# Three attention layers: scores of two units in one run, their maximum and difference in one VectorE operation each

## The reference

```
scores = einsum('bhid,bhjd->bhij', q, k) / sqrt(32)     # per sequence and head: 128 x 128
p      = softmax(scores)                                # layer 1: masked keys
out    = einsum('bhij,bhjd->bhid', p, v)                # layer 0: scaled per head, plus a field term
x      = x + out.reshape(B, S, E) @ Wo.T                # layer 1: normalised before it is added
```

## Time and profile before

| | us |
|---|---|
| median of 3 executions (2985.6 to 2991.92) | 2991.61 |
| the profiled execution's own time | 2992.51 |
| its span, first to last instruction | 2990.7 |
| TensorE busy | 2902.6 |
| VectorE busy | 2048.1 |
| ScalarE busy | 1367.8 |
| attention, about | 70 to 1896 |

### The profile page before, as it was taken

One profiled execution on the slowest core, in us unless ns is written; L12 is line 12 of the kernel. 1 busy time (PEld: TensorE's weight loads), 2 busy tenths in 40 slices (PEclk: granted clock), 3 DMA queues, 4 the chain that ended last, 5 costly groups with the idle time before them and its releaser, 6 DMA issues. The chain is left out here.

```text
span 2990.7 us, 69862 instructions
## 1 busy us (share of the span) xinstructions
PE 2902.6 (97%) x27255; PEld 2520.4 (84%) x27255; DVE 2048.1 (68%) x3640; ACT 1367.8 (46%) x2226; POOL 666.8 (22%) x563
## 2 busy tenths in 40 slices
PE   6999999999999999989999999899999999999998
PEld 5899999998888898878888888688888888888886
DVE  5788788876788888888777778654444465655554
ACT  3555545544566666656666666422222232222221
POOL 1222222221121111133222333122222221111111
PEclk8999999999999999999999999899999999999999
DMA  3444444457544444575443435411212240111101
GB/s 139 95 128 123 128 131 116 129 125 188 142 99 101 105 109 100 130 169 136 105 109 105 112 102 120 153 57 57 71 56 67 78 137 29 43 57 42 56 28 43
DMA packets 514586, 300.45 MB, mean 100 GB/s; under 512 B 411776, under 2 KB 484608, under 8 KB 513952
## 3 DMA queue, kind: packets, MB, share of 16 engines
q1 hardware_dynamic: 514464, 298.76, 37.4%
HBM read 139.31 MB, written 58.72 MB: 66 GB/s over the span
## 5 line engine op out<-in xcount | busy, mean ns | idle before, releaser
L747 PE MATMUL att_bank_a<-keep_hh,keep_wgateh 128*128 128x256 f32 x1536 | 453.1, 295 | 4.8 <-ACT att_af L913 2.3
L748 PE MATMUL att_bank_a<-keep_hh,keep_wgatel 128*128 128x256 f32 x1536 | 434.3, 283 | 0.0
L749 PE MATMUL att_bank_a<-keep_hl,keep_wgateh 128*128 128x256 f32 x1536 | 434.0, 283 | 0.0
L962 ACT ACTIVATE att_shifted<-att_shifted,keep_lift 128x512 f32<-128x512 f32 x384 | 276.6, 720 | 299.2 <-DVE att_shifted L1126 295.7
L1710 DVE TENSOR_TENSOR mlp_act_t<-mlp_bank_u,mlp_sg 128x512 f32<-128x512 f32 x128 | 88.5, 692 | 453.0 <-ACT mlp_sg L1616 449.3
L1122 DVE TENSOR_REDUCE att_top<-att_bank_s 128x4 f32<-128x512 f32 x384 | 264.1, 688 | 182.2 <-PE att_bank_s L798 180.8
L1759 POOL TENSOR_TENSOR mlp_al<-mlp_act_t,mlp_ah 128x512 fp32r<-128x512 f32 x128 | 174.9, 1367 | 870.3 <-ACT mlp_ah L1622 870.3
L1616 ACT ACTIVATE mlp_sg<-mlp_bank_g 128x512 f32<-128x512 f32 x128 | 76.6, 598 | 626.3 <-PE mlp_bank_u L1540 626.1
L957 ACT ACTIVATE att_pq<-att_shifted 128x512 f16<-128x512 f32 x384 | 241.2, 628 | 201.4 <-DMA att_pt<-att_pq 195.3
L747 PEld LDWEIGHTS att_bank_a<-keep_hh,keep_wgateh 128*128 128x128 f32 x1536 | 293.0, 191 | 16.4 <-DVE att_xres L1097 2.8
L748 PEld LDWEIGHTS att_bank_a<-keep_hh,keep_wgatel 128*128 128x128 f32 x1536 | 294.1, 191 | 0.1
(11 more groups left out here) (268 smaller groups left out, 7257.4 us busy)
## 6 DMA issues: line engine op xcount, KB each, us to landing
resid<-att_xres SPq DMA_DIRECT2D x47, 512.0 KB, 2.8
keep_xin<-resid SPq DMA_DIRECT2D x33, 512.0 KB, 3.8
mlp_res<-resid SPq DMA_DIRECT2D x32, 512.0 KB, 4.6
att_xres<-resid SPq DMA_DIRECT2D x31, 512.0 KB, 4.3
mlp_xf<-resid SPq DMA_DIRECT2D x30, 512.0 KB, 4.6
keep_xin<-in_x SPq DMA_DIRECT2D x16, 512.0 KB, 4.5
att_xres<-in_x SPq DMA_DIRECT2D x16, 512.0 KB, 3.8
keep_spare<-in_w_next SPq DMA_DIRECT2D x16, 512.0 KB, 3.9
```

What stands on the lines that cost most here:

```text
L747: nc.tensor.matmul(out, w_h, x_h, start=first, stop=False)
L748: nc.tensor.matmul(out, w_l, x_h, start=False, stop=False)
L749: return nc.tensor.matmul(out, w_h, x_l, start=False, stop=last)
L962: nc.scalar.activation(shifted[:, u % 2], shifted[:, u % 2], ACT.Exp, bias=k["lift"][:, 0:1], scale=SCALE).then_inc(exp_done, 1)
```

## The change

Two slots become one double slot d = 0 to 5; the two units of a double slot share one q/k chunk and differ in the sequence b.

- TensorE makes the scores of both units in one run of 24 matmuls into twice the columns of `bank_s`, in layer 1 behind 4 mask matmuls of 256 columns in place of 8 of 128. It waits once per pair for `shift_done` of the pair before. It weighs both units of a pair together, in all bodies (before: in layer 2 and in the last two groups of layers 0 and 1 one unit in each slot), at the head of double slots 2 to 5. The small jobs move behind the pieces of the even slot. `spans` is another list where there are 8 fills.
- VectorE takes the maximum of both units in one operation, and the difference in one; the difference waits for `low_probs` of both units of the pair before.
- ScalarE does exponential and high part of the first unit, then of the second.
- VectorE's list in a double slot: read the fills of the even slot, shift the pair, (d = 2: coherence factor), normalise the pair of d - 2, low part of the first unit, small jobs, read the fills of the odd slot, low part of the second unit, rest. `normalise(i, 3)` is now in d = 5 of its own group, and `add_field(i - 1, 1)` behind the first shift.
- The buffers stay as they are, and so do GpSimd's and SyncE's lists.

In the diff the first `for d` loop is ScalarE's, the second VectorE's.

```diff
+PAIRS = UNITS // 2
...
-        bank_s = ctx.enter_context(nc.psum_tensor("att_bank_s", [P, 4, 512], F32))[:, :, 0:P]
+        bank_s = ctx.enter_context(nc.psum_tensor("att_bank_s", [P, 4, 512], F32))[:, :, 0:NB * P]
...
-            spans = [2,2,1,1,2,2,2,2,2,2,1,1] if len(fills) == 10 else [2,2,1,1,1,2,2,1,1,1,1,1]
+            if len(fills) == 10:
+                spans = [2, 2, 1, 1, 2, 2, 2, 2, 2, 2, 1, 1]
+            else:
+                spans = [2, 2, 2, 2, 1, 1, 1, 1, 1, 1, 1, 1] if lay(i) < 2 else [2, 2, 2, 1, 2, 1, 1, 2, 1, 1, 1, 0]
...
+            def scores(i, c):
+                if positive(PAIRS * i + c):
+                    pe.wait_ge(shift_done, PAIRS * i + c)
...
+                for b in range(NB):
+                    at = slice(b * P, (b + 1) * P)
+                    for step, (q_t, k_t) in enumerate(((qh, kh), (qh, kl), (ql, kh))):
+                        for h in range(4):
...
+                            mm = nc.tensor.matmul(bank_s[:, h, at], q_t[rows, c, at], k_t[rows, c, at], ...
...
+                for s in range(0, SLOTS, 2):
...
+                        scores(i, s // NB)
                     if s >= 4:
+                        for u in (s - 4, s - 3):
                             weigh_values(i, u)
+                    if s == 6 and lay(i) == 0:
+                        sum_values(i, 0)
+                    if s == 10:
+                        turn_output(i, 0)
                     if not at_last:
                         project_pieces(pieces[s])
+                    if s == 0 and not (isinstance(i, int) and i == 0):
+                        turn_output(i - 1, 1)
+                    if s == 2 and lay(i) == 0:
+                        for b in range(NB):
+                            coherence(i, b)
+                    if norms(i) and s == 8:
+                        norm_sums(i)
+                    project_pieces(pieces[s + 1])
...
+                for d in range(SLOTS // 2):
+                    s = 2 * d
+                    if d == 0:
+                        for b in range(NB):
+                            first_values(i, b)
...
+                    read_fills(s)
+                    if d == 1 and has_x(i, 1):
+                        high_x(i + 1)
...
+                        for u in (s, s + 1):
+                            exponentials(i, u)
...
+                            high_probs(i, u)
+                    if d == 0 and positive(i):
+                        high_output(i - 1, 1)
...
+                    read_fills(s + 1)
+                    if d == 0:
                         for b in range(NB):
                             second_values(i, b)
+                    if d == (3 if post(i) else 2) and pre(i):
...
                         squares(norm_turn(1, i + 2), landing(i + 2))
...
+            def shift_scores(i, c):
+                n = PAIRS * i + c
+                src = bank_s.rearrange("p h (b j) -> p h b j", b=NB)
                 dve.wait_ge(s_full, n + 1)
+                nc.vector.reduce_max(top[:].rearrange("p b h -> p h b"), src, AX_X).then_inc(top_ready, 1)
                 dve.wait_ge(top_ready, n + 1)
+                if positive(NB * n):
+                    dve.wait_ge(p_low, NB * n)
+                peaks = top[:].rearrange("p b h -> p h b").unsqueeze(3).broadcast_to([P, 4, NB, P])
+                nc.vector.tensor_tensor(shifted[:].rearrange("p b h j -> p h b j"), src, peaks, ALU.subtract).then_inc(shift_done, 1)
...
+                for d in range(SLOTS // 2):
+                    s = 2 * d
+                    if s >= UNITS:
+                        normalise(i, d - 2)
+                    read_fills(s)
+                    if s < UNITS:
+                        shift_scores(i, d)
+                        if d == 0 and positive(i) and lay(i - 1) == 0:
+                            add_field(i - 1, 1)
+                    if d == 2 and lay(i) == 0:
+                        coherence_factor(i)
+                    if 2 <= d < PAIRS:
+                        normalise(i, d - 2)
+                    if s < UNITS:
+                        low_probs(i, s)
+                    if d == 0 and positive(i):
+                        low_output(i - 1, 1)
+                    if d == 1 and lay(i) == 0:
+                        coherence_sum(i)
...
+                    if d == 3 and post(i):
                         norm_gains(0, i - 1)
                         add_squares(0, norm_turn(0, i - 1))
...
+                    read_fills(s + 1)
+                    if s < UNITS:
+                        low_probs(i, s + 1)
+                    if d == 1 and has(i, 1) and lay(i + 1) == 0:
...
                         nc.vector.tensor_copy(tb[:], k["tanh_bias"][:, :, bass.ds(NB * (i + 1), NB)]).then_inc(tb_ready, 1)
```

More of the change, by code:

```diff
@@ L779, in project @@
                     mm.then_inc(a_full[bk], 1)
[L781 to L784, removed]
-                masked = lay(i) == 1
[L786 to L790, removed]
+            def scores(i, c):
+                if positive(PAIRS * i + c):
+                    pe.wait_ge(shift_done, PAIRS * i + c)
+                if c % 2 == 0:
+                    pe.wait_ge(a_free[0], a_done(i, ("k", c // 2)))
+                    pe.wait_ge(a_free[1], a_done(i, ("q", c // 2)))
+                masked = lay(i) == 1
                 if masked:
                     for h in range(4):
[L793 to L798, removed]
+                        out = bank_s[:, h, :].rearrange("p (b j) -> p b j", b=NB)
+                        nc.tensor.matmul(out, k["ident_b"][:], bcast_mid(k["mask"][:], NB), start=True, stop=False)
+                for b in range(NB):
+                    at = slice(b * P, (b + 1) * P)
+                    for step, (q_t, k_t) in enumerate(((qh, kh), (qh, kl), (ql, kh))):
+                        for h in range(4):
+                            rows = slice(HD * h, HD * (h + 1))
+                            mm = nc.tensor.matmul(bank_s[:, h, at], q_t[rows, c, at], k_t[rows, c, at], start=step == 0 and not masked,
+                                                  stop=step == 2 and (b == NB - 1 or not masked))
                 mm.then_inc(s_full, 1)
@@ L1030, in body, with read_fills @@
                 pieces = pieces_of(i)
-                for s in range(SLOTS):
-                    if s == 1 and positive(i):
-                        high_output(i - 1, 1)
-                    if s == 10:
-                        high_output(i, 0)
-                    if len(norms(i)) == 2 and s == 9:
-                        deviations(i)
+                def read_fills(s):
                     for fill in readable(pieces, s):
@@ L1067, in body @@
                         high_piece(piece_of(i))
-                    if s == 9 and isinstance(i, int) and i == ALL - 1:
+                    if d == 4 and isinstance(i, int) and i == ALL - 1:
                         first_weights_high()
@@ L1277, in body @@
-                    if s == 8 and lay(i) == 0:
+                for d in range(SLOTS // 2):
[17 more added lines that the diff above has]
+                        coherence_sum(i)
+                    if d == 1 and has(i, 1) and lay(i + 1) == 1:
+                        low_x(i + 1)
+                    if d == 3 and lay(i) == 0:
@@ L1286, in body @@
                         norm_start(i, 0, i - 1)
-                    if s == 9 and pre(i):
+                    if d == 4 and pre(i):
                         norm_start(i, 1, i + 2)
-                    if s == 10 and pre(i):
-                        norm_scale(1, i + 2)
-                    if s == 10 and piece_of(i) is not None:
-                        low_piece(piece_of(i))
-                    if s == 11 and post(i):
-                        for m in range(2):
-                            norm_add(i - 1, m)
@@ L1299, in body @@
                         nc.vector.tensor_copy(tb[:], k["tanh_bias"][:, :, bass.ds(NB * (i + 1), NB)]).then_inc(tb_ready, 1)
+                    if d == 4 and piece_of(i) is not None:
+                        low_piece(piece_of(i))
+                    if d == 5 and post(i):
+                        for m in range(2):
+                            norm_add(i - 1, m)
             iterate(dve, body)
```

125 lines of the change are left out of this document (46 added, 79 removed).

## The result

The changed kernel takes 3075.35 us (median of 4 runs, 3074.00 to 3076.54) against 2990.68 for the kernel before on the same chip: a ratio of 1.0286 [1.0268, 1.0304], 85 us slower. 3028 was forecast. The profiled execution took 3074.0, its span is 3072.2.

A forecast was written before the change was run, and what follows sets the result against it. TensorE was taken to pace the attention. Its waits less its savings gave +0.4, +0.6 and +1.2 us per group in layers 0, 1 and 2; times 16 groups, 35 us on 2992.5 made 3028 us, range 2945 to 3090.

The forecast's parts named there:

- TensorE's saving: Fewer changes between matmul kinds and wider masks take 1.0, 1.6 and 1.4 us per group off TensorE, 64 us in all.
- The loop from pair to pair: VectorE's shift, ScalarE's exponentials and high parts, and the last low part run in sequence: 5.8 us bare per pair.
- Layer 2: Per group, TensorE loses 2.9 us in waits, gains 1.4, and 0.3 of earlier stall is already inside: +1.2.
- Layer 1: Per group, TensorE wants the last transposes at 28.5 but gets them at 30.7; loses 2.2, gains 1.6: +0.6 us.
- The walk: Stepping through the engines' lists of one group, from the end of the first pair's scores, to find TensorE's waits.
- Layer 0: Per group, TensorE loses 1.4 us at `turn_output` and the second value pair, gains 1.0: +0.4.
- GpSimd's hold on unit 1: Unit 1's VectorE low part stands until the first of two GpSimd operations ends, done at 8.5 in layer 2's group.
- The layer ends: The groups at the ends of layers, taken as unchanged by the forecast, as was the MLP.
- The rival of the clock: Stalls in layers 1 and 2 drop TensorE to 1.2 GHz, 1.5 us in each of 32 groups: +48, 3076; chance 0.10.
- GpSimd keeps the port: GpSimd holds through both operations, unit 1's low part 1.04 us later per group: +50, 3078 us; chance 0.12.
- the rule for two inputs: VectorE instructions with two SBUF inputs and GpSimd ones reading SBUF block each other; 0.81 and 2.35 us rows cited.
- TensorE's saving comes through: Layer 1's 15.4 us chain from pair 2's scores to last transpose fits TensorE's 13.6: 2923 to 2985 us; chance 0.25.

The follow-up runs named there:

- Experiment 12: Experiment 1's kernel with `add_field(i - 1, 1)` ahead of the group's first maximum and layer 2's dummy square root ahead of ScalarE's fill reads: 2929.55 us.
- experiment 1: The changed kernel, but VectorE takes maximum and difference of each unit separately and ScalarE starts at the first unit's difference: 2957.29 us.
- experiment 2: Experiment 1's kernel with one wait changed: ScalarE's first exponential of a pair waits for both units' differences: 3112.76 us.
- experiment 6: The changed kernel with one more VectorE operation per group, a second copy of `low_output(i, 0)` into an unread tile: 3088.62 us.
- experiment 7: The changed kernel with VectorE's `low_x` moved ahead of unit 2's low part in layer 1: 3069.37 us.
- experiment 4: The changed kernel with the last piece of q0 computed twice in layer 1, 12 more TensorE matmuls per group: 3073.16 us.
- experiment 9: The changed kernel with GpSimd's low part of the coherence operand (`low_t`) cut to 16 of 256 columns from the second group on: 3068.56 us.
- experiments 8: The changed kernel with two GpSimd steps mostly left out, the values' third part and the coherence operand's low part: 3034.76 us.

## Why the prediction was right or wrong

**The direction was right, and so was the mechanism in part.** VectorE's double operations take 1.22 us, the table copy 0.16 (0.2 forecast), a score run to the next instruction 0.82 (0.83), ScalarE's waits for transposes fell from 195 to 10 us, and the low part of unit 1 takes 1.45 to 1.52 us. TensorE waits where it was said to: at value runs for `att_of`, at `turn_output` in layer 0, at the banks of k and q. Experiment 12 shows that TensorE's saving is real and even larger: 1.34, 1.54 and 1.86 us, 76 over the layers for the 64 forecast. The loop from pair to pair was there too: 5.8 us bare by forecast, 6.4 to 6.5 between the later maxima of a group in layer 1. Experiments 1 and 2 show that the late release in it is what gave the saving back. Why it cost 85 us and not 35 is another matter: in whole layers the excess over the forecast is 17, 27 and 4 us.

**Layer 2 was sized right as a sum**, +1.35 for +1.2, its two parts less so: the saving is 1.9 instead of 1.4, and the waits cost 35.81 - 32.25 = 3.6 instead of 2.9.

**Layer 1: the step that failed** is "TensorE has, from 14.9, ... 13.6: it wants it at 28.5. Loses 2.2, gains 1.6". It takes the period as TensorE's list plus its stalls, up to the last value pair. The walk stops there and leaves out what VectorE still owes: `normalise`, `norm_scale`, `low_output` and `norm_add`, done at 1072.59 in the rows of experiment 6, 5.6 us behind the end of that value run (1067.02); TensorE has the next scores done 4.5 behind it (1071.54). Nor does it have `low_x` ahead of the low part of unit 3, of which 0.5 was in the way (37.82 to 37.36 in experiment 7), nor the 1.63 us scaling. TensorE, which was to lose 2.2 and gain 1.6, stands still for 3.29 with the clock at 1.00. So it was VectorE's turn that closed the loop, and the period was +1.96 instead of +0.6: 22 us over the 16 groups.

**Layer 0: the hold by `low_t` was put at nothing.** I had priced GpSimd's hold on unit 1 only. That on unit 5 (1.78 us instead of 0.69) makes shift 3 and ScalarE's read of the tanh bank late, a stall of 0.82 that I didn't have; without the two GpSimd steps the period is 41.96, 0.16 above before. Forecast +0.4, measured +1.73: 21 us.

**The layer ends** "I take as unchanged". They were not: in layer 1, 16 of the 37 us lie in five of its 16 distances (the first and the last four), 3.1 each against 1.96 in the middle, with stalls of 1.2 to 3.4 us where the kernel before had up to 2.3. Which waits make this up was not tried one by one, and the cause of this part stays open.

**The rival of the clock** forecast 3076, and 3075 was measured: that is luck. It had the clock fall in 32 groups of layers 1 and 2. It falls in 6 of the steady groups of layer 1, 4 of layer 0 and none of layer 2 (1.00 from 1440 to 1900 us), and in the steady groups it costs 2 us, all in layer 0: in layer 1 groups with and without it take the same time, and experiment 4 gives the clock back and gains nothing. A time that fits a rival is no proof of it. **GpSimd keeps the port** was wrong as a rival for the changed kernel (unit 1's low part ends after the first of the two operations, 1.45 to 1.52), yet the two steps' holds are worth 41 us. Of the two rows that the prediction sets beside the rule for two inputs, only that of 0.81 us bears on it: the copy of 2.35 us has one input, as the held scaling has one besides its factor. **TensorE's saving comes through** had it that the chain would have to be 2.2 us per group shorter: 1.17 us less before ScalarE's start, four times a group, is what did it in experiment 1.

## What to carry to other kernels

When two engines hand work to each other, merging the first one's operations moves the second one's start from after the first part to after the last. Count that per hand-over, and beside the time the merge saves: here 1.17 us lost for 0.16 gained. The Trainium skill, "VectorE: DVE Perf Modes", section "Rules for kernel authors", advises to keep the number of VectorE operations small; by that rule the changed kernel should beat experiment 1, and by the runs it is 118 us slower. The rule holds for VectorE's own time (experiment 2 against the changed kernel) and not for who waits. Merge on the engine that has nobody waiting inside the merged piece (TensorE's runs), keep separate what releases someone.

Close the loop before pricing it: follow each engine's list from one group's start to the next one's. The pace is set by the longest such way round, and the idle time of any other engine, a lowered clock included, is then a remainder and no cost (layer 1 here; in layer 0, where TensorE binds, the lowered clock did cost). A cheap test is to add a known operation and see whether the period grows by it.

## What the runs showed of the hardware that was not expected

TensorE's granted clock went to 0.5 behind the same stall of 1.72 us in 6 groups of layer 1 and not in 5 others, and behind stalls of 1.21 us in 5 of 12 groups of layer 0 (experiment 9). Stalls of 1.09 and 1.26 us (layer 1 of experiments 8 and 7) left it at 1.00. So the length of the one stall doesn't decide it alone.

A GpSimd operation can hold a VectorE operation of 8 elements for 1.4 us (1.63 instead of 0.23, rows behind experiment 7). Of two GpSimd operations back to back VectorE's low part of unit 1 was let in behind the first; but in layer 2 of experiment 1 unit 0's, begun while GpSimd was at work on eight small operations ahead of them, took 2.88 us and ended 0.56 behind the second:

```profile
1593.64 2.88 DVE L1139 TENSOR_TENSOR att_pq<-att_shifted,att_pq 128x512 f16<-128x512 f32 x1 [0.21 <-ACT att_pq L959]
...
1593.75 2.21 POOL L1342 TENSOR_TENSOR att_vr<-att_vf,keep_v 128x512 f32<-128x512 f32 x2
```

One maximum or difference over 1024 elements out of PSUM takes 1.22 us against twice 0.68 or 0.69, but the dependent one starts 1.34 behind the maximum (0.71 for 512): doubled operations save VectorE 0.16 us per pair.

The kernels of experiments 1 and 2 issue the same instructions on every engine and differ by 155 us, 5%, by one wait.
